# Causal mask of the attention scores: four products over 32 rows each in place of four over 128 rows

## The reference

```python
x = x + attn(layernorm(x), W_qkv, W_out)
x = x + xattn(layernorm(x), ctx, ctx, ...)
x = x + ffn(layernorm(x), ...)

def attn(x, W_qkv, W_out):
    q, k, v = split(einsum('bsd,ndh->bnsh', x, W_qkv))
    attn = einsum('bnqh,bnkh->bnqk', q, k) * head_dim ** -0.5
    mask = -1e10 * (1.0 - tril(ones((S, S))))
    attn = softmax(attn + mask, axis=-1)
    out = einsum('bnqk,bnkh->bnqh', attn, v)
    ...
```

## Time and profile before

| | |
|---|---|
| three executions | 990.99, 987.38, 990.98 us |
| profiled execution, first to last instruction | 996.1 us |
| granted TensorE clock, mean over it | 0.953 |
| TensorE busy | 890.7 us, 89% |
| VectorE, ScalarE, GpSimd busy | 606.8, 486.2, 526.7 us |
| mask products, line 617 | 192, 39.8 us busy |

### The profile page before, as it was taken

The page is one execution under the profiler, slowest core; times in us unless marked ns, Lnnn a source line. Parts: engine busy times, 40 slices in busy tenths (PEclk is TensorE's granted clock), DMA queues, the critical chain, the costliest instruction groups (busy, mean ns, idle before and its releaser), DMA issues.

```text
span 996.1 us, 31655 instructions
## 1 busy us (share of the span) xinstructions
PE 890.7 (89%) x11877; PEld 661.9 (66%) x11966; DVE 606.8 (61%) x1340; ACT 486.2 (49%) x810; POOL 526.7 (53%) x660
## 2 busy tenths in 40 slices
PE   4799999999997687899989888899999999999995
PEld 3566666667665354656656576687787878787783
DVE  4767778677675445776767667455555555555552
ACT  3567677677666356455555544233333333333331
POOL 2556657557555334387777767543444434353442
PEclk9999999999997789788888999999999999999998
DMA  9112443443435643444445323332323323232221
GB/s 288 52 45 54 112 114 81 108 114 80 117 104 117 161 154 101 130 150 146 162 149 166 116 65 88 83 76 49 50 46 54 50 44 53 47 51 49 50 34 22
DMA packets 133198, 92.97 MB, mean 93 GB/s; under 512 B 75712, under 2 KB 114112, under 8 KB 132928
## 3 DMA queue, kind: packets, MB, share of 16 engines
q1 hardware_dynamic: 119760, 73.10, 26.3%
q0 software_dynamic: 13296, 17.83, 10.3%
HBM read 54.65 MB, written 37.32 MB: 92 GB/s over the span
## 4 chain that ended last, share of the span: by engine, by line
PE 62%; DVE 10%; DMA 6%; ACT 6%; issue 5%; POOL 4%; SPq 3%; another core or an unknown queue 1%; DVEq 0%; POOLq 0%; ACTq 0%
PE pair L951 18%; PE pair L965 9%; PE pair L967 7%; PE pair L644 4%; PE pair L666 3%; PE pair L680 3%; PE pair L822 3%; DMA o_scr<-On 2%; DMA STG<-wup_in 2%; POOL sm L1571 2%; PE pair L617 2%; DVE SD L1147 2%; PE pair L693 2%; ACT PT L1348 2%; PE pair L836 2%
## 5 line engine op out<-in xcount | busy, mean ns | idle before, releaser
L951 PE MATMUL pair<-XTs,WU 128*128 128x128 bf16 x3408 | 285.5, 220 | 12.8 <-issue 6.0
L951 PEld LDWEIGHTS pair<-XTs,WU 128*128 x3408 | 238.6, 98 | 82.3 <-issue 19.3
L1608 POOL DMA_INDIRECT out_d<-XB x71 | 115.4, 1625 | 212.6 <-DVE XB L1313 189.0
L1484 ACT ACTIVATE Hf<-pair 128x512 f32<-128x512 f32 x142 | 84.8, 598 | 222.6 <-PE pair L951 210.7
L965 PE MATMUL pair<-WD,Hh 128*128 x479 | 181.6, 380 | 0.0
L1304 DVE CAST Hh<-Hf 128x512 bf16<-128x512 f32 x142 | 64.5, 454 | 172.4 <-ACT Hf L1484 158.9
L967 PE MATMUL pair<-WD,Hl 128*128 x568 | 155.0, 273 | 5.3 <-issue 0.5
L1529 POOL TENSOR_SCALAR_AFFINE_SELECT PT<-PT 128x512 f32<-128x512 f32 (+1 forms) x96 | 74.7, 792 | 56.5 <-ACT PT L1342 51.1
L1306 DVE TENSOR_TENSOR Hl<-Hf,Hh 128x512 bf16<-128x512 f32 x142 | 99.8, 703 | 4.9
L1037 DVE TENSOR_REDUCE mxn<-pair 128x4 f32<-128x1024 f32 x64 | 75.3, 1218 | 26.7 <-PE pair L625 26.6
L1147 DVE TENSOR_TENSOR SD<-pair,SD 128x1024 f32<-128x1024 f32 x48 | 58.7, 1223 | 51.5 <-ACT SD L1426 28.7
(11 more groups left out here) (241 smaller groups left out, 1804.3 us busy)
## 6 DMA issues: line engine op xcount, KB each, us to landing
XB<-xs_scr SPq DMA_DIRECT2D x71, 130.0 KB
STG<-wup_in SPq DMA_DIRECT2D x32, 256.0 KB, 4.5
q_scr<-SPL SPq DMA_DIRECT2D x16, 512.0 KB, 4.2
STG<-wdn_in SPq DMA_DIRECT2D x32, 256.0 KB, 2.7
o_scr<-On SPq DMA_DIRECT2D x32, 128.0 KB, 4.1
Mm<-o_scr SPq DMA_DIRECT2D x16, 256.0 KB, 2.8
CnT<-ctxt_in SPq DMA_DIRECT2D x16, 256.0 KB, 4.2
CX<-ctx_in SPq DMA_DIRECT2D x16, 256.0 KB
```

The source lines that it names most:

```text
L951: t = e.matmul(upb(j, k)[:, 128 * (fm % 4):128 * (fm % 4) + 128], WU[:, bass.ds(reg[j] * 4096 + off, 128)], XTs[:, r, hx, dk, :], start=n ...
L1484: e.activation(Hf[:, r, hs], upb(j, k), ACT.Gelu).then_inc(gel.sem, 1)
L1608: e.indirect_dma_start(out=out, out_offset=bass.IndirectOffsetOnAxis(ap=XS[:, i % NX, 256:257].bitcast(I32), axis=0), in_=Yf[:, i % NY, :] ...
```

## The change

The mask of the scores is made from two factors of 31 rows of powers of two (and one row of zeros), which repeat on each of the four groups of 32 partitions and come from DRAM as a new input `msk` of 64 KB. Bank jj of pair u gets its mask from the rows 64u + 32jj to 64u + 32jj + 31. The product of the factors is strongly negative over the diagonal, close to nothing under it, and -64 on the diagonal; it enters only the row maxima. The old `mkb` moves to the same memory: VectorE writes it over the first factor when the last S0 is done, at the start of the mLSTM stage, and `dsel` takes the place of the second factor.

```diff
+        LM = sb("LM", [128, 2, 128], BF)
+        mkb = LM[:, 0, :]
-        mkb = sb("mkb", [128, 128], BF)
-        dsel = sb("dsel", [128, 2, 32], F32)
+        dsel = LM[:, 1, :].bitcast(F32).rearrange("p (a c) -> p a c", a=2)
...
                     out_ = [pair_of(kind, *key, u) for u in range(2)]
+                    w.wait_ge(l_lm, 16)
                     for u in range(2):
                         pair_free(w, kind, *key, u)
                         for jj in range(2):
-                            e.matmul(out_[u][:, jj, :].rearrange("p (g c) -> p g c", c=wd)[:, :, wd - 128:wd], idb[:, :],
-                                     mkb[:, :].rearrange("p (a c) -> p a c", a=1).broadcast_to([128, n, 128]),
+                            rows = slice(64 * u + 32 * jj, 64 * u + 32 * jj + 32)
+                            e.matmul(out_[u][:, jj, :].rearrange("p (g c) -> p g c", c=wd)[:, :, wd - 128:wd], LM[rows, 0, :],
+                                     LM[rows, 1, :].rearrange("p (a c) -> p a c", a=1).broadcast_to([32, n, 128]),
                                      start=True, stop=False, skip_group_check=True)
...
                         pair_left(w, 1)
+                        w.wait_ge(b_init, 1)
...
             e.tensor_copy(idb[:, :], idf)
-            e.tensor_copy(mkb[:, :], CF[:, C_MASK:C_MASK + 128])
...
+            w.wait_ge(s0m.sem, s0m.at(B - 1, 1))
+            e.tensor_copy(mkb, CF[:, C_MASK:C_MASK + 128])
             link(e.memset(dsel[:, :, :], 0.0))
...
             load_x(0)
+            e.dma_start(LM[:, :, :].bitcast(F32).rearrange("p a c -> p (a c)"), msk).then_inc(l_lm, 16)
             e.dma_start(WQf[:, :, 0:512], wqkv[:, :, 0:512]).then_inc(l_w[0], 16)
...
+def causal_factors():
+    a, b = np.zeros((32, 128), np.float32), np.zeros((32, 128), np.float32)
+    n = np.arange(128)
+    blk, off = n // 6, n % 6
+    sup, pos = blk // 5, blk % 5
+    for r in range(22):
+        a[r, blk == r] = np.exp2(66.0 - 24.0 * off[blk == r])
+        b[r, blk == r] = -np.exp2(24.0 * off[blk == r] - 60.0)
+    for r in range(5):
+        a[22 + r, sup == r] = np.exp2(60.0 - 31.0 * pos[sup == r])
+        b[22 + r, sup == r] = -np.exp2(31.0 * pos[sup == r] - 62.0)
+    for r in range(4):
+        a[27 + r, sup == r] = np.exp2(60.0)
+        b[27 + r, sup > r] = -np.exp2(40.0)
...
```

More of the change, by code:

```diff
@@ L243, in of, with build @@
     return [s[1:] for s in steps if s[0] == kind]
-def build(nc, x, ctx_in, ctx_t, wqkv, wout, wg, bg, gain, wr, br, wup, wdn, cst, out):
+def build(nc, x, ctx_in, ctx_t, wqkv, wout, wg, bg, gain, wr, br, wup, wdn, cst, msk, out):
     xs = nc.dram_tensor("xs_scr", (XROWS, ROW), F32, kind="Internal").ap()
@@ L380, in build @@
         dvc, poc = Chain(sem("dve_chain")), Chain(sem("pool_chain"))
+        l_lm = sem("l_lm")
         l_c, l_w, l_wo, l_wg, l_z = sem("l_c"), (sem("l_w0"), sem("l_w1")), sem("l_wo"), sem("l_wg"), sem("l_z")
@@ L796, in tensor_mlstm @@
                     for g in range(2):
-                        e.matmul(ZD[:, g, :].rearrange("p (a c) -> p a c", a=n)[:, :, 0:128], mkb[:, :],
+                        e.matmul(ZD[:, g, :].rearrange("p (a c) -> p a c", a=n)[:, :, 0:128], mkb,
                                  idb[:, :].rearrange("p (a c) -> p a c", a=1).broadcast_to([128, n, 128]),
@@ L1820, in _ @@
                     experts(g)
-_INS = ["x", "ctx", "ctxt", "wqkv", "wout", "wg", "bg", "gain", "wr", "br", "wup", "wdn", "cst"]
+_INS = ["x", "ctx", "ctxt", "wqkv", "wout", "wg", "bg", "gain", "wr", "br", "wup", "wdn", "cst", "msk"]
 def constants():
@@ L1850, in constants @@
     return c
+def causal_factors():
+    import numpy as np
+    a, b = np.zeros((32, 128), np.float32), np.zeros((32, 128), np.float32)
[11 more added lines that the diff above has]
+        b[27 + r, sup > r] = -np.exp2(40.0)
+    words = np.stack([np.tile(v, (4, 1)) for v in (a, b)], 1).astype(np.float32).view(np.uint32) >> 16
+    return np.ascontiguousarray(words.astype(np.uint16)).reshape(128, 256).view(np.float32)
 def layout(inputs):
@@ L1865, in layout @@
               "bg": i["L0_xattn_ifgate_b"], "gain": i["L0_xattn_outnorm_w"].reshape(2, 128).T, "wr": wr, "br": i["L0_ffn_router_b"],
-              "wup": wup, "wdn": wdn, "cst": constants()}
+              "wup": wup, "wdn": wdn, "cst": constants(), "msk": causal_factors()}
     return {n: np.ascontiguousarray(a) for n, a in arrays.items()}
```

## The result

The changed kernel takes 992.0 us (median of 20 runs, 986.6 to 996.4), the kernel before 987.0 us in 20 runs on the same chip (982.4 to 991.0). The ratio is 1.004, with a 95% interval of 1.0023 to 1.0058: slower by 5.0 us, where 3.8 us less were forecast. The time lies inside the range, but the sign is the other one, and a ratio of 1 lies outside the interval. (The ratios here are those on record, with their intervals; they are not the quotient of the two medians, which is 1.005 here.) The forecast of 987.2 us started from the median of three runs of before, 990.98 us; from the 987.0 us of twenty runs, 3.8 us less would have been 983.2 us. The profiled execution has a span of 989.2 us. That of before was 996.1 us, longer than any of the 20 runs of its kernel, so the two spans don't show the loss, and stages have to be compared.

The account below looks back on a forecast made before the run. TensorE was taken to bound most of each of attention's thirteen iterations. Gains of 9 x 0.43 + 0.08 + 0.17 = 4.1 us, less 0.3 for the start, gave 990.98 - 3.8 = 987.2 us, range 980.5 to 993.0.

Parts of the forecast that it names:

- S1 of half 0: Mask products before TensorE's wait at T0: they end 0.43 us sooner, TensorE waits 0.43 us longer for VectorE; gain zero.
- rival D: Clock falls in longer pauses, as before T0 of half 0; two iterations at half clock give about 999 us; chance 0.08.
- S1 of half 1: Mask products between PV and QK, where nothing else is waited for: the whole steady gain, 0.43 us for each iteration.
- The price of a mask: Four 256-column mask products on 32 rows instead of 128, judged by line 649: from 0.54 to 0.11 us.
- S0: Mask products ahead of VX: worth 0.0, since the key copy and ScalarE's exponential hold TensorE; 0.43 us without that cover.
- The other loop: Transfers and GpSimd's scale for QN: 0.43 us less slack each iteration; two late ones gain nothing, nine others have enough slack.
- Rival C: The transfer loop binds in more than half of the iterations, leaving 1 to 2 us: about 989.9 us; chance 0.20.
- The start: One more transfer issued ahead of the weights, which ScalarE waits for: costs 0.3 us, bounds 0.0 and 0.64.
- The passage: Into the mLSTM: step D waits for b_init, 2.1 us late; the resulting 1.1 us lie beside the chain, so no cost.
- A: TensorE is the bound throughout attention: each of 16 batches gives 1.79 us, so 962.4 us; chance 0.04.
- B: The second half of S0 gains too: 0.86 us an iteration, so 983.3 us; chance 0.16.
- E: The factors' products do not run side by side: no gain, the start costs 0.3, so 991.3 us; chance 0.05.

Follow-up runs that it names:

- e1: The changed kernel, but the mask of S1 of half 0 is again four 128-row products; ratio to the kernel before 0.9983.
- e4: The changed kernel with only the S1 of half 1 mask on 32 rows, the other masks on 128 rows; ratio to the kernel before 0.9985.
- e6: The changed kernel with only the S0 mask on 32 rows, both S1 masks on 128 rows; ratio to the kernel before 1.0009.
- e8: The kernel before, unchanged, profiled a second time; no ratio given, reaches the T0 that ends the ten iterations at 290.96 us.
- e5: The changed kernel with only the S1 of half 0 mask on 32 rows, the others on 128; 998.3 against 990.6 us before, ratio 1.0102.
- e11: The changed kernel, all masks on 32 rows, with GpSimd's weight split moved behind QN's scale and the factors' transfer issued later; ratio to the kernel before 1.0027.
- e2: The changed kernel, all masks on 32 rows, but each product of S1 of half 0 issued four times; ratio to the kernel before 0.9986.
- e9: e7 with GpSimd's first weight split moved behind the scale that QN needs; 992.8 against 999.2 us for the kernel before, ratio 0.9949.
- e7: The changed kernel with S1 of half 1 on 32 rows, S0 on 128, S1 of half 0 on 128 and issued twice, factors' transfer later; ratio to before 0.9977.
- e12: The changed kernel with all masks on 128 rows, those of S1 of half 0 issued twice, factors' transfer later; ratio to the kernel before 1.0042.
- e10: Control for e9: all masks on 128 rows and issued once, GpSimd's split moved, factors' transfer later; ratio to the kernel before 0.9988.

## Why the prediction was right and wrong

**The step that failed** is *S1 of half 0* with its "Zero", together with the argument under rival D that "the waits of 1.57 us left the clock at 1.00". TensorE does wait longer for VectorE there, and that time is free in the sense of the chain. It wasn't free for the clock. The usual wait rose from 1.04 to 1.38 us, and the clock fell in five of thirteen iterations. I had taken one isolated wait of 1.57 us as proof for a wait that comes in every iteration. It wasn't proof even for a single one: among sixteen single waits of 1.31 to 1.57 us in the ten iterations of before, e1 to e4, e6 and e8, two have a fall right behind them (e4 at 194.31, e6 at 101.75), while of the thirty T0 of half 0 in the ten iterations of after, e5 and e11, where 1.38 us is the usual wait, fourteen have one (from 0.2 us ahead of T0's start, in the pause, to 1.2 us behind it). e1 and e2 fill that pause and the five falls go; e5 makes that pause alone and the falls come, with 1.0102.

**Rival D** had the right mechanism and place, with a chance of 0.08, and a wrong size. I priced an iteration at half clock at some 6 us. A fall lasts through part of an iteration only and costs 19.60 - 17.97 = 1.63 us; five of them cost 8.1 us, against a gain of about 5.6 us.

The Trainium skill's page "TensorE: Matmul & The Clock Gate", section Why this matters for your kernels, which stood beside rival D, advises against pauses between bursts of products, since they bring the half clock back, and it speaks of longer pauses than any before T0 here. The trace of after agrees in kind, in attention too, with 0.50 at 103 to 105 us, but behind a pause of only 1.82 us, and elsewhere of 1.38; for the length the measured pauses decide.

**The sum by the runs.** The mean granted clock is 0.942 over the 20 runs of the changed kernel and 0.953 over 35 runs of before (on the chip of e1). With rows at 1.00 and 0.50, half clock for a share f of the span lowers the mean by f/2, so after has 2 x 0.011 x 990 = 22 us more of it. A fall in the table costs 1.63 us for 2 x 0.09 x 19.6 = 3.5 us at half clock (the steps of 1 us above add up to 3.4), so 22 us cost about 10 us, an estimate. Less 13 x 0.44 = 5.7, and with 0.3 for the start, that leaves 4.8 us slower; 5.0 were measured. That the falls outside the ten iterations cost at the same rate is assumed; in the profile of after the five falls are 17 us at half clock, and another of 6.8 us lies at the start. e5 gives a second case: 0.9408 against 0.9507 is 20 us more at half clock, 9 us by the same rate and no gain, and 7.8 us were measured. In e1 and e4 the mean clock is 0.949 against 0.953, by the same sum some 3.4 us lost. With 5.7 gained and 0.3 for the start they would be 2.0 us faster; 1.5 and 1.0 were measured. So the small loss of clock fits their shortfall, though no trace shows where it lies. e11 doesn't fit: 0.936 against 0.951 would cost 15 us against a gain of 5.7, and it is 3.0 us slower than before. The sum is a rough one, and the runs of e1, e2, e5 and e11 carry the verdict.

**What was right.** *S1 of half 1*: 0.43 us forecast, 0.44 found, in after, e1, e2, e4 and e9. *The price of a mask*, from the 32-row row beside it: 0.11 us. *S0*: zero, by e6, with ScalarE's two waits in view. *The other loop*: five late `QN` in after, seven in e7 and nine in e1 after four in before; e9 shows what it held back. That the nine other iterations have enough slack was too hopeful: once the falls are gone, as in e1, the loop takes some of the gain (the ten iterations of e1 are 3.1 us shorter than before, not 4.4). Rival C has its mechanism there, but not the deciding one in after. *The start*: the first mask comes at 18.32 us where it came at 17.99, 0.33 us late against 0.3 forecast. A fall of the clock between 20 and 27 us follows in that profile, and T0 of half 0 that opens the thirteen iterations comes at 49.88 us where it came at 48.40, 1.48 us late. In e5, with the same transfer and no fall at the start, it comes at 48.73, again 0.33 late; in e8, the kernel before with a fall at the start, at 50.31. So the transfer costs about what was forecast, and the rest comes with the falls at the start. These aren't tied to it: five of seven profiles with the early transfer have one before 48 us, and four of the seven others. For the 0.33 us the size was right and the place wasn't: the first weight copy comes no later (8.21 us, where it came at 8.30) and doesn't wait for its transfer, ScalarE's row:

```profile
8.21 1.04 ACT L1336 ACTIVATE WQh<-PT 128x1024 bf16<-128x1024 f32 x1
```

The delay is already in ScalarE's first `xn` (7.21 us, before 6.99), which waits for GpSimd's scale and not for the weights. *The passage* is hidden, as forecast.

Rivals A, B and E are excluded. A and B need 17.6 us or less for an iteration, and nine of the ten take 17.97 or more; the last was shorter before too (267.60 to 285.42, 17.82 us) and takes 17.38, again 0.44 less. Against E, the four products of S1 take 0.11 us to the scores behind them, as those of line 649 did.

**The numbers.** The forecast had 0.43 us for iterations that were all warm. That 992.0 us lies inside the range, near its upper end, is no success of the mechanism: the gain per iteration was there and the falls outweighed it.

## What to carry to other kernels

Time taken off TensorE pays only where TensorE is what the next step waits for; taken off in front of a wait it makes the wait longer, and that isn't neutral, because a longer pause in each turn of a loop can halve the clock of the products behind it. Read the usual wait as well as the longest one, since one long wait that passed without a fall proves little, and look at the granted clock by iteration, since a page in 40 slices hides falls of a few microseconds. Where such a pause is left, harmless products into a bank that is overwritten anyway may keep the clock (e2: four narrow ones for one; in e12, where nothing else was gained, such products went with a kernel 0.4% slower, for a cause that is open), and the order of the other loops must be mended with it before the gain shows (e7 against e9).

## What the hardware showed that I had not expected

- A change of the usual pause before T0 from 1.04 to 1.38 us is enough to take the falls of the clock from 0 or 1 in ten iterations (before, e1 to e4, e6, e8, e10) to 4 or 5 in ten (after, e5, e11). Of single pauses of 1.31 to 1.57 us, two in sixteen had a fall right behind them.
- An iteration loses 1.63 us for 3.4 us at half clock, a little under half. Nearly all of it is in the PV products, which go from 2.81 to 4.37 us.
- The kernel before has such falls itself now and then (e8: 6.8 us at half clock and an iteration of 20.63 us).
- Four 32-row bf16 products of 256 columns side by side cost 0.11 us, where four 128-row ones cost 0.54.
